# A state-space stage on one Trainium2 core: a normalization later, a copy earlier, and a prefetch's gathers split over two places

## The chip, the cores and the metric

The kernel runs on one core of a Trainium2 chip. The metric is the device time of one execution in microseconds (us), lower is better. Several executions are timed and their median is taken. One further execution was recorded by the hardware profiler, and all profile rows are from that one.

## What is computed

A two-layer decoder over `x` of 16 x 256 x 256 floats: differential attention, cross attention and a mixture of experts, then a state-space block, causal cross attention and a feed-forward block, each with a residual sum and a layer norm. The change is inside the state-space block, which is, cut to what matters:

```python
def _L1_attn_ref(x, in_proj_w, conv_w, conv_b, norm_w, out_proj_w, dt_bias, A_log, D_param):
    zxbcdt = jnp.einsum('bld,ed->ble', x, in_proj_w)
    z, xBC, dt = ...            # 512, 512 + 2 * 128 and 8 columns
    xBC = silu(causal convolution with 4 taps of xBC + conv_b)
    x_part, B_part, C_part = ...
    dt = jax.nn.softplus(dt + dt_bias)
    A = -jnp.exp(A_log)
    # for every token t: state = state * exp(A * dt_t) + (x_t * dt_t) B_t;  y_t = state C_t
    _, y_seq = lax.scan(step, state0, inputs)
    y = y + x_part * D_full
    y = y * jax.nn.silu(z)
    y = y * jax.lax.rsqrt(jnp.mean(y * y, axis=-1, keepdims=True) + EPS) * norm_w
    return jnp.einsum('ble,de->bld', y, out_proj_w)

x = _layernorm(x + _L0_ffn_ref(x, ...))     # its last sum and norm are done by this stage
x = _layernorm(x + _L1_attn_ref(x, ...))
```

## The kernel before

Each engine has one program written out by hand; an engine executes its instructions strictly in that order, and semaphores (`wait_ge`, `then_inc`) tie the engines together. The stages follow one another; the one edited here is `state_space` (L2169). In the trace its tiles carry the prefix `ssm_`.

The stage works on 16 blocks of 256 tokens (two tiles of 128 rows, `QT` = 2). The scan over tokens is not done token by token: in a block of 256 it is a product with a lower triangular matrix of decays, which is made on the fly. Every engine runs the same loop `for n in STEPS`, n from -7 to 16. In step n the core computes the state-space mix of block n, the output of block n - 1, and prepares later blocks: the projections of the next pair of blocks (eleven units B, C, x0, x1, x2, dt, x3, z0 to z3 per pair, six in an even step, five in an odd one), the transposition of block n + 4, the sum of the experts of block n + 5, and the load of block n + 7. In the loop, `now` says that block n exists, `late` that block n - 1 does, and `soon` that block n + 1 does.

The parts that the prediction speaks of, by engine:

- **PE** (TensorE): `project`, `state_products`, `exponents(n, 0..5)` (sums of logarithms that become decays, L2391 and L2392), `output(n - 1)`, `mix` (L2417 to L2419), `transpose_x`, `turn_steps` (L2360). `exponents(n, u)` for u of 2 or more waits for `decays(n, u - 2)`, as the bank of PSUM has to be free. A projection's bank is free when the unit two before it has been read.
- **ACT** (ScalarE): `decays(n, u)` (L2535) takes the exponential of a bank of exponents into tile `mat[u]`; `first_tap` (L2554) the first tap of the convolution; `normalize_x(n + 4)` (L2596) applies the layer norm to the sum of experts with `c_shift` and `c_rstd`; `normalize_y(n - 1)` (L2624) does so with the finished rows and `shift`; `copy_steps` (L2523) takes the dt unit to SBUF, for PE to turn it; `tails` (L2529) is a small exponential.
- **DVE** (VectorE): `sum_experts(n + 5)` (L2732, L2739 and the moments), `masked_products` (L2804), three more taps for each unit (L2758), the multiplications of `mat` 0, 2 and 4 with the mask (L2692), `tail_rows` (L2812), `high_terms` (L2795), `mean_squares` (L2827), `residual(n - 1)` (L2836).
- **POOL** (GpSimd): the multiplications of `mat` 1, 3 and 5 (L2692), `scale_rows` (L2985), the low terms `rhs_lo` (L2992), `scale_y` and `scale_x` (L2962 to L2967, four small instructions each, whose last one writes `shift` and `c_shift`), `split_y` (L3002, tile `y_lo`), and `gather(n + 7)` (L2954): four indirect DMAs that fetch the two routed experts' rows of a block of 256 tokens, two for each expert.

A gather's tile has three copies, and block b's gather waits until the sum of block b - 3 has been made. `sum_experts(b)` waits for all four of its block. SP (SyncE) loads the shared expert's rows of each block and stores the finished rows; it is not edited.

## Time and profile before

| | us |
|---|---|
| median of 3 runs | 2781.28 |
| lowest and highest run | 2781.17 and 2789.03 |
| the profiled execution's own time | 2787.02 |
| its span in the trace | 2784.9 |
| state space, steps 0 to 13 (starts of PE's state products, 1756.5 and 2070.4) | 313.9 |

The span is what the profiler saw from the first instruction to the last; 2.1 us lie around it. The mean granted TensorE clock over the span was 0.933 of full speed. Steps 0 to 15 lie between 1756.5 and about 2135 us of the span.

### The profile page before, as it was taken

How to read it: one execution, taken by the hardware profiler on the slowest of the kernel's cores; microseconds unless marked ns; L12 is line 12 of the kernel's file. 1: busy time of each engine (PE TensorE's matmuls, PEld its weight loads, DVE VectorE, ACT ScalarE, POOL GpSimd, SP SyncE). 2: the span in 40 equal slices, each digit the busy share in tenths (PEclk: the TensorE clock that was granted, in tenths of full speed). 3: DMA queues.
4: the chain of work that ended last, by engine and by line, in shares of the span. 5: the costliest groups of instructions: out<-in, count | busy, mean ns of one | idle time of the engine just before them, and what ended most of it. 6: DMA issues, size and time to landing. Idle time of an engine off the chain costs nothing. (4 is left out here: it accounts for less than half of the span.)

```text
span 2784.9 us, 66303 instructions
## 1 busy us (share of the span) xinstructions
PE 2455.1 (88%) x24760; PEld 2025.6 (73%) x24760; DVE 1921.6 (69%) x3087; ACT 1434.1 (51%) x2247; POOL 1564.4 (56%) x1871
## 2 busy tenths in 40 slices
PE   4899999999599998798999994888896799996998
PEld 3677666676466665798999993677775577775998
DVE  2566666677358877263888885999985377775776
ACT  2566555565246665333665663656663356553333
POOL 3565665666334553036666664777764577763443
PEclk8899999999789999799999997999997799998999
DMA  7555555552377784124666663111100877751111
GB/s 180 130 146 130 141 142 127 142 147 68 93 202 202 196 207 103 36 73 148 215 229 220 230 218 116 46 31 46 31 12 21 231 209 202 214 146 35 57 56 49
DMA packets 229623, 364.07 MB, mean 131 GB/s; under 512 B 53536, under 2 KB 158752, under 8 KB 221856
## 3 DMA queue, kind: packets, MB, share of 16 engines
q1 hardware_dynamic: 208832, 281.87, 37.7%
q0 software_dynamic: 17376, 78.13, 8.0%
q8 instruction: 153, 2.51, 0.4%
q10 hardware_dynamic: 3200, 1.05, 0.2%
q14 instruction: 62, 0.51, 0.1%
HBM read 232.27 MB, written 133.69 MB: 131 GB/s over the span
## 5 line engine op out<-in xcount | busy, mean ns | idle before, releaser
L1243 ACT ACTIVATE self_probs<-self_score_ps 128x768 f32<-128x768 f32 x256 | 207.4, 810 | 217.7 <-PE self_score_ps L1145 214.4
L1451 POOL TENSOR_SCALAR_AFFINE_SELECT self_probs<-self_probs 128x512 f32<-128x512 f32 x256 | 167.2, 654 | 217.7 <-ACT self_probs L1243 215.1
L1372 DVE TENSOR_REDUCE self_neg_max<-self_max_ps 128x2 f32<-128x256 f32 x256 | 108.0, 422 | 227.6 <-PE self_max_ps L1131 224.5
L685 DVE TENSOR_REDUCE cross_neg_max<-cross_max_ps 128x4 f32<-128x1024 f32 x128 | 156.0, 1222 | 73.1 <-PE cross_max_ps L473 71.2
L601 ACT ACTIVATE cross_probs<-cross_score_ps 128x1024 f32<-128x1024 f32 x128 | 131.0, 1024 | 93.3 <-PE cross_score_ps L495 93.0
L1373 DVE TENSOR_REDUCE self_neg_max<-self_max_ps 128x2 f32<-128x512 f32 x256 | 174.2, 680 | 0.0
L2160 POOL TENSOR_TENSOR moee_h_lo<-moee_h,moee_h_hi 128x512 fp32r<-128x512 f32 x78 | 112.0, 1436 | 92.0 <-ACT moee_h_hi L1897 91.2
L3458 POOL TENSOR_TENSOR ffn_g_lo<-ffn_g_full,ffn_g_hi 128x512 fp32r<-128x512 f32 x64 | 82.2, 1284 | 129.0 <-ACT ffn_g_hi L3344 116.6
L1145 PE MATMUL self_score_ps<-self_q_stack,self_k_stack 49*128 49x128 f32 (+1 forms) x1024 | 131.6, 336 | 23.9 <-issue 10.2
L1897 ACT ACTIVATE moee_h_hi<-moee_h 128x512 fp32r<-128x512 f32 x110 | 69.5, 632 | 160.9 <-DVE moee_h L2063 160.9
L601 ACT ACTIVATE causal_probs<-causal_score_ps 128x768 f32<-128x768 f32 x128 | 103.8, 811 | 92.1 <-PE causal_score_ps L495 92.0
L79 PE MATMUL moee_g_ps<-moee_x_hi,moee_in_hi 128*128 128x256 f32 x440 | 132.1, 300 | 9.7 <-DVE moee_x_lo L2050 5.5
L1145 PEld LDWEIGHTS self_score_ps<-self_q_stack,self_k_stack 49*128 49x128 f32 x1024 | 79.1, 191 | 73.0 <-issue 40.1
L1125 PE MATMUL self_max_ps<-self_k_stack,self_q_stack 48*128 48x128 f32 (+1 forms) x1024 | 108.7, 292 | 26.4 <-POOL self_k_stack L1482 25.5
L2063 DVE TENSOR_TENSOR moee_h<-moee_u_ps,moee_silu 128x512 f32<-128x512 f32 x110 | 75.5, 686 | 80.9 <-PE moee_u_ps L81 76.5
L2103 POOL DMA_INDIRECT x_tiles<-kept_x,moek_slot x64 | 65.2, 1019 | 109.7 <-issue 104.9
L80 PE MATMUL moee_g_ps<-moee_x_lo,moee_in_hi 128*128 128x256 f32 x440 | 126.5, 287 | 0.0
L81 PE MATMUL moee_g_ps<-moee_x_hi,moee_in_lo 128*128 128x256 f32 x440 | 126.5, 287 | 0.0
L775 POOL TENSOR_SCALAR_AFFINE_SELECT causal_probs<-causal_probs 128x512 f32<-128x512 f32 x128 | 85.6, 669 | 71.8 <-ACT causal_probs L601 68.0
L79 PE MATMUL moee_y_ps<-moee_out_hi,moee_h_hi 128*128 128x256 f32 x440 | 125.2, 284 | 0.7 <-DVE moee_out_lo L2015 0.7
L79 PE MATMUL moee_u_ps<-moee_x_hi,moee_in_hi 128*128 128x256 f32 x440 | 125.5, 285 | 0.0
L81 PE MATMUL moee_u_ps<-moee_x_hi,moee_in_lo 128*128 128x256 f32 x440 | 125.0, 284 | 0.0
(488 smaller groups left out, 9659.9 us busy)
## 6 DMA issues: line engine op xcount, KB each, us to landing
self_q<-self_q_split SPq DMA_DIRECT2D x48, 512.0 KB, 3.2
self_q_raw<-self_q SPq DMA_DIRECT2D x32, 768.0 KB, 7.4
cross_stacks<-cross_qk SPq DMA_DIRECT2D x64, 384.0 KB
causal_stacks<-causal_qk SPq DMA_DIRECT2D x64, 384.0 KB
moe_y_tiles<-moee_y SPq DMA_DIRECT2D x55, 256.0 KB, 2.4
x_tiles<-zeros SPq DMA_DIRECT2D x16, 624.0 KB, 4.5
moee_xT<-x_tiles SPq DMA_DIRECT2D x39, 256.0 KB, 7.2
cross_qk<-cross_k_split SPq DMA_DIRECT2D x16, 512.0 KB, 3.9
```

Of the source, the lines that this page charges most:

```text
L79: pe.matmul(out, a[0], b[0], start=start, stop=False, **kw)
L80: pe.matmul(out, a[0], b[1], start=False, stop=False, **kw)
L81: return pe.matmul(out, a[1], b[0], start=False, stop=stop, **kw)
L601: nc.scalar.activation(probs[i // 2][:, a, :, lo:], score_ps[:, :, lo:], ACT.Exp, scale=HD ** -0.5).then_inc(prob_ready, 1)
L685: last = dve.tensor_reduce(neg_max[p][:, tile, :, col % 4, :], bank[:].rearrange("p a (q k) -> p a q k", q=QT), AX.X, ALU.max, negate=True)
L1125: last = pe.matmul(max_ps[i % 2][:, ab, q * S:q * S + (q + 1) * P], q_stack[rows, 4 * tile + c, q * P:(q + 1) * P], k_stack[p][rows, tile, ...
L1145: last = pe.matmul(score_ps[:, ab, j * S + k * P:(j + 1) * S], k_stack[p][rows, tile, k * P:(k + 1) * P], q_stack[rows, 4 * tile + c, k * P:],
L1243: nc.scalar.activation(probs[g % 4][:, a, :, P:], score_ps[:, :, P:], ACT.Exp, scale=HD ** -0.5).then_inc(prob_ready, 1)
L1372: dve.tensor_reduce(neg_max[:, tile, :, c, 0:1], bank[:, :, 0:P], AX.X, ALU.max, negate=True)
L1373: dve.tensor_reduce(neg_max[:, tile, :, c, 1:2], bank[:, :, S:2 * S], AX.X, ALU.max, negate=True).then_inc(max_kept, 1)
L1451: pool.affine_select(diagonal, diagonal, [[0, 2], [0, 2], [1, P]], ALU.is_ge, zero, base=0, channel_multiplier=-1).then_inc(prob_masked, 1)
L2160: pool.tensor_tensor(h_lo[p][f][:].rearrange("p j s -> p (j s)"), h[f][:], h_hi[p][f][:].bitcast(F32).rearrange("p j s -> p (j s)"), ALU.s ...
```

## The change

It edits the order of the instructions of ACT and POOL in the state space. None is added or taken away, and no semaphore's count changes.

- **ACT, even steps:** `normalize_x(n + 4)` moves from ahead of `decays(n, 1)` to behind `first_tap(n, 2)`. `tails` goes from behind `decays(n, 2)` to ahead of it. `copy_steps(n)` goes ahead of `normalize_y(n - 1)`.
- **POOL, even steps with n of 0 or more:** of the four indirect DMAs of `gather(n + 7)`, the two of the first expert go between `mat` 3 and `mat` 5, the other two between the low terms and `scale_y`. They were last in the step.
- **POOL, odd steps with n of 0 or more:** the first two go behind `mat` 5, the other two to the end of the step, behind `split_y`. All four were between the second `rhs_lo` and `scale_x`.

```diff
--- before.py
+++ after.py
@@ -2632,14 +2632,14 @@
                     if now:
                         decays(n, 0)
                     first_tap(n, 1)
+                    if now:
+                        decays(n, 1)
+                        tails(n)
+                        decays(n, 2)
+                        decays(n, 3)
+                    first_tap(n, 2)
                     if real(n + 4):
                         normalize_x(n + 4)
-                    if now:
-                        decays(n, 1)
-                        decays(n, 2)
-                        tails(n)
-                        decays(n, 3)
-                    first_tap(n, 2)
                     if now:
                         decays(n, 4)
                     first_tap(n, 3)
@@ -2651,9 +2651,9 @@
                     if now:
                         upper_y(n)
                         square_y(n)
+                    copy_steps(n)
                     if late:
                         normalize_y(n - 1)
-                    copy_steps(n)
                 else:
                     if now:
                         decays(n, 0)
@@ -2945,10 +2945,12 @@
             pool.memset(neg_half[:], -0.5).then_inc(half_set, 1)
             pool.wait_ge(half_set, 1)
 
-            def gather(b):
+            def gather(b, ks=range(TOP)):
+                if not real(b):
+                    return
                 if b >= 3:
                     pool.wait_ge(sum_ready, b - 2)
-                for k in range(TOP):
+                for k in ks:
                     for q in range(QT):
                         c = b * QT + q
                         pool.indirect_dma_start(y_routed[b % 3][:, k, q, :], None, y_tiles,
@@ -3013,12 +3015,15 @@
                     matrices(pool, n, 3, high_mat_ready)
                 if n % 2 == 0:
                     if now:
+                        gather(n + 7, (0,))
                         matrices(pool, n, 5, high_mat_ready)
                     if late:
                         scale_rows(n - 1)
                     if n >= 0 and soon:
                         low_terms(n + 1, 0)
                         low_terms(n + 1, 1)
+                    if now:
+                        gather(n + 7, (1,))
                     if late:
                         scale_y(n - 1)
                     if real(n + 5):
@@ -3026,13 +3031,14 @@
                     if now:
                         split_y(n, 0)
                         split_y(n, 1)
-                    if real(n + 7):
+                    if not now:
                         gather(n + 7)
                 else:
                     if late:
                         scale_rows(n - 1)
                     if now:
                         matrices(pool, n, 5, high_mat_ready)
+                        gather(n + 7, (0,))
                     if n == -5:
                         scale_x(n + 5)
                     if n == -3:
@@ -3043,13 +3049,15 @@
                         scale_y(n - 1)
                     if soon:
                         low_terms(n + 1, 1)
-                    if real(n + 7):
+                    if not now:
                         gather(n + 7)
                     if n >= -1 and real(n + 5):
                         scale_x(n + 5)
                     if now:
                         split_y(n, 0)
                         split_y(n, 1)
+                    if now:
+                        gather(n + 7, (1,))
                     if n == -1:
                         lower_wo()
 
```

On POOL, from the end of step 2 into step 3 (odd) there stood before: `y_lo` of step 2, the four gathers, `mat` 1 and 3 of step 3, the scale of the rows, `mat` 5 and a low term:

```order
L3002 TENSOR_TENSOR ssm_y_lo<-ssm_yz,ssm_y_hi 128x512 x2
L2954 DMA ssm_y_routed<-moe_y_tiles,moek_slot 128x256 x4
L2692 TENSOR_TENSOR ssm_mat<-ssm_mat,ssm_gm 128x512 x2
L2985 TENSOR_TENSOR ssm_row_scale<-ssm_ms,ssm_neg_half 128x2
L2692 TENSOR_TENSOR ssm_mat<-ssm_mat,ssm_gm 128x512
L2992 TENSOR_TENSOR ssm_rhs_lo<-ssm_triang,ssm_a_lo 128x1024
```

The same place after the change (lines of this part of the file lie two further down):

```order
L3004 TENSOR_TENSOR ssm_y_lo<-ssm_yz,ssm_y_hi 128x512 x2
L2692 TENSOR_TENSOR ssm_mat<-ssm_mat,ssm_gm 128x512 x2
L2987 TENSOR_TENSOR ssm_row_scale<-ssm_ms,ssm_neg_half 128x2
L2692 TENSOR_TENSOR ssm_mat<-ssm_mat,ssm_gm 128x512
L2956 DMA ssm_y_routed<-moe_y_tiles,moek_slot 128x256 x2
L2994 TENSOR_TENSOR ssm_rhs_lo<-ssm_triang,ssm_a_lo 128x1024
```

Four gathers are gone from ahead of `mat` 1 and 3, and two stand behind `mat` 5.

On POOL, from the end of step 3 into step 4 (even), before, from `shift` on:

```order
L2967 TENSOR_TENSOR ssm_shift<-ssm_low,ssm_rstd 128x2
L2992 TENSOR_TENSOR ssm_rhs_lo<-ssm_triang,ssm_a_lo 128x1024
L2954 DMA ssm_y_routed<-moe_y_tiles,moek_slot 128x256 x4
L2962 TENSOR_SCALAR ssm_c_var<-ssm_c_mv 128x2
L2963 TENSOR_SCALAR ssm_c_low<-ssm_c_mv 128x2
L2965 TENSOR_TENSOR ssm_c_rstd<-ssm_c_var,ssm_neg_half 128x2
L2967 TENSOR_TENSOR ssm_c_shift<-ssm_c_low,ssm_c_rstd 128x2
L3002 TENSOR_TENSOR ssm_y_lo<-ssm_yz,ssm_y_hi 128x512 x2
L2692 TENSOR_TENSOR ssm_mat<-ssm_mat,ssm_gm 128x512 x3
```

And after the change:

```order
L2969 TENSOR_TENSOR ssm_shift<-ssm_low,ssm_rstd 128x2
L2994 TENSOR_TENSOR ssm_rhs_lo<-ssm_triang,ssm_a_lo 128x1024
L2964 TENSOR_SCALAR ssm_c_var<-ssm_c_mv 128x2
L2965 TENSOR_SCALAR ssm_c_low<-ssm_c_mv 128x2
L2967 TENSOR_TENSOR ssm_c_rstd<-ssm_c_var,ssm_neg_half 128x2
L2969 TENSOR_TENSOR ssm_c_shift<-ssm_c_low,ssm_c_rstd 128x2
L3004 TENSOR_TENSOR ssm_y_lo<-ssm_yz,ssm_y_hi 128x512 x2
L2956 DMA ssm_y_routed<-moe_y_tiles,moek_slot 128x256 x2
L2692 TENSOR_TENSOR ssm_mat<-ssm_mat,ssm_gm 128x512 x2
L2956 DMA ssm_y_routed<-moe_y_tiles,moek_slot 128x256 x2
L2692 TENSOR_TENSOR ssm_mat<-ssm_mat,ssm_gm 128x512
```

The four instructions of `scale_x` have no gather ahead of them any more; two of step 3's gathers stand between `y_lo` and `mat` 1, and two of step 4's between `mat` 3 and `mat` 5.

On ACT, an even step, as a piece of the difference: the two normalizations (L2596) fall from the second place to behind the tap of x0 (L2554 of `ssm_xs`).

```order
 L2535 ACTIVATE ssm_mat<-ssm_e_ps 128x512
 L2554 ACTIVATE ssm_bc<-ssm_in_ps,ssm_cb,ssm_cw 128x512
+L2535 ACTIVATE ssm_mat<-ssm_e_ps 128x512
+L2529 ACTIVATE ssm_tail<-ssm_g_ps 128x8
+L2535 ACTIVATE ssm_mat<-ssm_e_ps 128x512 x2
+L2554 ACTIVATE ssm_xs<-ssm_in_ps,ssm_cb,ssm_cw 128x512
 L2596 ACTIVATE ssm_x<-ssm_x,ssm_c_shift,ssm_c_rstd 128x256 x2
-L2535 ACTIVATE ssm_mat<-ssm_e_ps 128x512 x2
-L2529 ACTIVATE ssm_tail<-ssm_g_ps 128x8
-L2535 ACTIVATE ssm_mat<-ssm_e_ps 128x512
-L2554 ACTIVATE ssm_xs<-ssm_in_ps,ssm_cb,ssm_cw 128x512
```

Three `decays`, `tails` and one tap pass the normalization.

## Rows read from the trace of the kernel before

**Rows 1.** The page, part 1: busy us, share of the span, instructions

```profile
PE 2455.1 (88%) x24760; PEld 2025.6 (73%) x24760; DVE 1921.6 (69%) x3087; ACT 1434.1 (51%) x2247; POOL 1564.4 (56%) x1871
```

**Rows 2.** Stretches: us, busy us (instructions) of PE, PEld, DVE, ACT, POOL; PEclk; DMA; GB/s

```profile
1851.50:1876.90 25.40, 21.68 (x151) 18.04 (x150) 24.56 (x44) 11.67 (x19) 16.75 (x18) 0.93 0.10 29
1876.90:1901.60 24.70, 22.24 (x161) 19.08 (x159) 23.53 (x45) 18.64 (x31) 21.73 (x23) 1.00 0.21 63
...
1952.60:1979.10 26.50, 22.79 (x151) 18.89 (x150) 24.64 (x44) 11.65 (x19) 16.66 (x18) 0.87 0.08 23
...
2003.80:2027.30 23.50, 21.63 (x151) 18.04 (x149) 22.49 (x44) 11.51 (x19) 13.16 (x13) 0.93 0.00 1
```

These are the steps 4, 5, 8 and 10.

**Rows 3.** Waits from 1760 to 1970 us: total us, times, longest

```profile
PE ssm_e_ps L2391 <- ACT ssm_mat L2535: 16.8, 5, 3.8
...
ACT ssm_x L2596 <- POOL ssm_c_shift L2967: 7.3, 4, 2.1
```

**Rows 4.** Timeline of POOL, step 4: start, us, instruction [idle before]

```profile
1849.93 1.88 POOL L2954 DMA_INDIRECT ssm_y_routed<-moe_y_tiles,moek_slot  x1 [0.16 <-issue]
...
1854.81 0.95 POOL L2954 DMA_INDIRECT ssm_y_routed<-moe_y_tiles,moek_slot  x1 [0.30 <-issue]
...
1857.25 0.18 POOL L2967 TENSOR_TENSOR ssm_c_shift<-ssm_c_low,ssm_c_rstd 128x2 f32<-128x2 f32 x1
...
1866.47 1.37 POOL L2692 TENSOR_TENSOR ssm_mat<-ssm_mat,ssm_gm 128x512 f32<-128x512 f32 x1 [3.19 <-ACT ssm_mat L2535]
...
1876.36 0.22 POOL L2962 TENSOR_SCALAR ssm_var<-ssm_mv 128x2 f32<-128x2 f32 x1 [2.90 <-issue]
```

**Rows 5.** Timeline of ACT, step 4

```profile
1857.47 1.09 ACT L2596 ACTIVATE ssm_x<-ssm_x,ssm_c_shift,ssm_c_rstd 128x256 f32<-128x256 f32 x2 [1.74 <-POOL ssm_c_shift L2967]
1858.47 1.06 ACT L2535 ACTIVATE ssm_mat<-ssm_e_ps 128x512 f32<-128x512 f32 x2
```

**Rows 6.** Timeline of PE, step 4

```profile
1859.09 0.50 PE L2391 MATMUL ssm_e_ps<-ssm_rhs_hi,ssm_one_r 128*128 128x512 f32 x1 [3.72 <-ACT ssm_mat L2535]
```

**Rows 7.** Timeline of DVE, steps 4 and 5, then step 11

```profile
1859.55 2.58 DVE L2692 TENSOR_TENSOR ssm_mat<-ssm_mat,ssm_gm 128x512 f32<-128x512 f32 x2
1862.06 1.76 DVE L2812 TENSOR_TENSOR ssm_xdt_tail<-ssm_xdt,ssm_tail 128x512 f32<-128x512 f32 x1
...
1884.50 1.26 DVE L2692 TENSOR_TENSOR ssm_mat<-ssm_mat,ssm_gm 128x512 f32<-128x512 f32 x2
1885.68 0.69 DVE L2812 TENSOR_TENSOR ssm_xdt_tail<-ssm_xdt,ssm_tail 128x512 f32<-128x512 f32 x1
...
1888.57 2.38 DVE L2692 TENSOR_TENSOR ssm_mat<-ssm_mat,ssm_gm 128x512 f32<-128x512 f32 x1
...
2031.26 3.50 DVE L2692 TENSOR_TENSOR ssm_mat<-ssm_mat,ssm_gm 128x512 f32<-128x512 f32 x2
...
2038.65 0.68 DVE L2692 TENSOR_TENSOR ssm_mat<-ssm_mat,ssm_gm 128x512 f32<-128x512 f32 x1
```

**Rows 8.** Timeline of step 5: gathers, `mat`, low term on POOL; two waits of PE; DVE; ACT

```profile
1882.47 1.09 POOL L2954 DMA_INDIRECT ssm_y_routed<-moe_y_tiles,moek_slot  x1 [0.16 <-issue]
...
1887.85 2.54 POOL L2692 TENSOR_TENSOR ssm_mat<-ssm_mat,ssm_gm 128x512 f32<-128x512 f32 x2
...
1893.69 1.90 POOL L2992 TENSOR_TENSOR ssm_rhs_lo<-ssm_triang,ssm_a_lo 128x1024 fp32r<-128x1024 f32 x1 [0.90 <-DVE ssm_a_lo L2789]
...
1879.61 0.41 PE L2360 MATMUL ssm_in_ps<-ssm_ident,ahead_front 8*128 8x8 f32 x4 [0.78 <-ACT ahead_front L2523]
1891.10 0.40 PE L2417 MATMUL ssm_y_ps<-ssm_mat,ssm_xdt_tail 128*64 128x128 f32 x2 [1.61 <-DVE ssm_mat L2692]
...
1891.63 0.88 DVE L2836 SCALAR_TENSOR_TENSOR ssm_y_out<-ssm_xT_ps,ssm_row_scale,ssm_x 128x256 f32<-128x256 f32 x2 [0.68 <-issue]
...
1897.96 1.09 ACT L2624 ACTIVATE ssm_y_out<-ssm_y_out,ssm_shift,ssm_rstd 128x256 f32<-128x256 f32 x2 [0.64 <-POOL ssm_shift L2967]
```

**Rows 9.** Timeline of DVE, step 8

```profile
1965.71 2.36 DVE L2795 TENSOR_TENSOR ssm_rhs_hi<-ssm_triang,ssm_a_hi 128x1024 fp32r<-128x1024 f32 x2 [0.79 <-PE ssm_e_ps L2392]
```

## Prediction

> **What bounds the kernel now.** The page comes first: PE is busy 88% of the span and VectorE (DVE) 69% [rows 1]. Those are averages over five stages, so the stage that is edited has to be read by itself. It is the state space, and within it the steps n = 0 to 15, one block of 256 tokens each. I cut the trace at the instant at which PE starts the state products of each step. The table by stretches then shows what the reader should see [rows 2]: step 4 takes 25.4 us, of which DVE works 24.56 and PE 21.68; step 5 takes 24.7 us with DVE at 23.53. Step 2 is like step 4 (25.6 us), step 6 like step 8 (26.3 and 26.5 us), and steps 3, 5, 7 and 9 take 24.7 us each. DVE has under 2 us of idle time in any of them. So DVE is the engine that is full, and the granted TensorE clock is below 1.00 in the even steps alone.
>
> Then the waits of that stretch. ScalarE (ACT) waits four times, 7.3 us in all, for `c_shift`, which GpSimd computes, and PE waits five times, 16.8 us in all, for `mat`, which ACT computes [rows 3]. In order of time it is one chain, here in step 4. GpSimd issues the four gathers of block 10 from 1849.93 to 1855.76 and computes `c_shift` of block 8 only then, until 1857.43 [rows 4]. ACT can normalize block 8 only from 1857.47 and takes 1.09 us, and behind that stand `decays` 1 and 2 [rows 5]. PE's next exponents need `decays` 1, and start after 3.72 us of waiting, at 1859.09 [rows 6]. The granted clock is 0.93 over step 4 and 0.87 over step 8, and 1.00 over step 5 [rows 2]: a part of the even steps runs at 1.2 GHz and not at 2.4, behind the place at which PE stood still.
>
> Last, DVE's own rows, because a full engine can be full of waiting. DVE and GpSimd hold each other up when both read two tiles of SBUF. `mat` 4 of step 5 takes DVE 2.38 us, while the same instruction in step 11 takes 0.68; GpSimd worked on its own `mat` tiles at the first time [rows 7, 8]. The pair in step 4 takes 2.58 where the pair in step 5 takes 1.26, and the `xdt_tail` product 1.76 against 0.69 [rows 7]. That is 1.7 us in an odd step and 1.3 + 1.1 = 2.4 us in an even one, recorded as DVE work.
>
> The Trainium skill, page "SBUF — State Buffer", section "Who interferes with whom", says that a DVE instruction with two SBUF inputs and a GpSimd instruction that reads SBUF exclude each other for a whole instruction; by that rule, these rows agree.
>
> **The change, part by part.**
>
> *Normalization of x later on ACT (even steps).* It moves behind `decays` 1 to 3, `tails` and the first tap of x0. No instruction is added. `decays` 1 then start when their exponents and ACT are ready, right after the tap of C, and not at 1858.47, behind the wait: PE's 3.72 us wait mostly goes, and with it the slow clock. But PE is not the full engine. PE then runs up against DVE: the projection of x1 needs the taps of C, which DVE ends at 1859.55 in any case. What DVE itself gets back is its idle time. In step 8 DVE waits 0.79 us for PE's last exponents, since these came at the slow clock [rows 9]; step 6 shows 0.80 at the same place. Step 10 gathers nothing and its ACT finds `c_shift` ready; it takes 23.5 us with all of DVE's other work in it, the sum of experts included [rows 2]. It is the nearest row to what an even step becomes. I take 23.9, 0.4 us above it, since the second half of an odd step's gathers now stands right ahead of GpSimd's `mat` 1, so that it may still meet DVE's pair (as it did for 0.3 us in step 10, and for 1.3 in step 4). Steps 2, 4, 6 and 8: 1.7 + 1.5 + 2.4 + 2.6 = 8.2 us. The bounds for each: nothing, if all the collisions stay, and 2.4 + 0.4 = 2.8 us, if all go.
>
> *Gathers in the even steps.* The first pair goes between `mat` 3 and `mat` 5, where GpSimd idles 3.19 us, the second behind the low terms, where it idles 2.90 us [rows 4]. A gather is 0.95 us and 0.30 of issue, so a pair is 2.5 us and fits in either gap. Beside a DVE product of two SBUF inputs a gather took 1.88 us [rows 4]; a pair at that price is 4.4 us and makes `mat` 5 up to 1.2 us late. PE has the whole output product of the block before and the first `mix` ahead of its use, so I cost both pairs at nothing. That cover would be gone if `mat` 5 came later than DVE's `mat` 4 and the first `mix` behind it.
>
> The Trainium skill, page "SBUF — State Buffer", infers in the same section that a DVE tensor-tensor product does not hold up the building of a gather's descriptors. The 1.88 us row speaks against it; by the page the pair would be 2.5 us everywhere, and the sum the same.
>
> *Gathers gone from between `y_lo` and `mat` 1 (odd steps).* They took 5.4 us there, and pushed `mat` 3 onto DVE's `mat` 4. Without them `mat` 1 and 3 run some 4 us earlier, `mat` 4 on DVE falls back towards 0.68, and PE's 1.61 us wait for it goes [rows 7, 8]. Up to 1.7 us, and with DVE's 0.68 of idle behind it 2.4 us. Against that stand new meetings: step 11, the odd step without gathers, has the pair at 3.50, where step 5 has 1.26 [rows 7]. Step 11 has no sum of experts between `y_lo` and the pair, so the meeting is milder with one, but not gone. Between +2.4 and -2.2 us (3.50 less 1.26) a step I take +0.7, nearer to the gain, since in steps 3 to 9 the sum of experts keeps DVE away from its pair until GpSimd is nearly through `y_lo`.
>
> *Gathers placed behind `mat` 5 (first pair) and at the step's end (second pair), odd steps.* GpSimd waits 0.90 us for `a_lo` there [rows 8]; the pair takes 2.5, so the low terms, `shift` and all behind them come up to 1.6 us later. `mat` 5 comes about as much earlier, as no gathers stand ahead of it. ACT waits 0.64 us for `shift` already [rows 8]. I count nothing, with 1.6 us as the bound. Past the second pair, `c_shift` comes before the gathers and not behind them: that is the other half of the cure for ACT's wait. The gathers land a few us after issue and their sums come two steps later, so no DMA is late. SP's queue is not touched.
>
> *Steps copied ahead of the finished rows.* PE waits 0.78 us in each odd step for ACT's copy, which stood behind a 1.09 us normalization and its wait [rows 8]. The copy now comes up to 1.5 us earlier. DVE reads the turned steps only when it is free, which it was not: nothing.
>
> *Steps 0, 1 and 10* have parts of the same: 1.0 us in all.
>
> **The sum.** 8.2 + 4 x 0.7 + 1.0 = 12.0 us. Against the profiled execution's own 2787.0 us that is 2775.0. The profiled execution stood 5.7 us above the median of the three runs, 2781.3, so for the median 2781.3 - 12.0 = 2769.3 us, 0.4% less. Two of three runs lie at 2781 and one at 2789. About 0.3%, 8.3 us, is what a measurement of this kernel can tell from no change.
>
> **The rivals.**
>
> *The collisions only move.* DVE stays full, and what it no longer loses at one product it loses at the next. For it: DVE has hardly any idle time in steps 2 to 9, and step 11 has more blocked time without the gathers than step 5 with them. Against it: step 10 is 1.9 us shorter than step 4 [rows 2]. Then only the slow clock's share is won, 1.0 us in steps 6 and 8 each, and some 0.5 us in the other even steps: 4 us, 2777.3 us. Chance 0.30.
>
> *Slower: the early pair delays the turn of the step.* If `mat` 5 of the odd steps is not earlier (because `row_scale` ahead of it waits for DVE's mean squares, at the same time as before), the first pair's 1.6 us go to `shift`, then to ACT's last two gates, which free PE's banks, and to `y_lo`, which then meets the next step's sums for another 1.1 us. 2.7 us in each of steps 3, 5, 7 and 9, against 1 us won in steps 6 and 8 each: +9 us, 2790 us. It decides where `low_terms` start more than 0.9 us later behind `a_lo` than now. Chance 0.08.
>
> *Both kinds of collision go.* Each even step gives 2.8 us, steps 6 and 8 another 1.0 for the slow clock, each odd step 2.4, and steps 0, 1 and 10 together 1.2: 4 x 2.8 + 2.0 + 4 x 2.4 + 1.2 = 24 us, 2757 us. For it: the lengths of the bare products [rows 7]. Against it: GpSimd has 17 to 22 us of work in every step, and most of it reads two tiles. Chance 0.10.
>
> **How the numbers follow.** My forecast, between 9 and 17 us less, has 0.52. Faster by over 0.3% is this and the last rival: 0.62. Within 0.3% is the first rival: 0.30. Slower is the second: 0.08. The likeliest case gives 2769.3. The range runs from 2757, the case with no collisions, to 2783, which takes in the first rival and a run or two from the upper end of its spread; about 0.15 is left out.
>
> **What would show it.** Right: PE's wait for `mat` in even steps 2 to 8 at under 1.5 us, granted clock 1.00 in them, no wait of ACT for `c_shift`, even steps near 24 us, odd ones near 24. The two halves are told apart by DVE's `mat` 4 in odd steps: near 0.7 us if the gathers' place helps, near 2.4 if not. It would be wrong if the even steps stay above 25 us although PE's wait is gone (DVE then holds the pace), or if ACT's wait for `shift` in odd steps grows above 2 us.

## The result, and the profile after

The changed kernel has a median of 2793.6 us over six runs (2791.1 to 2796.5). The kernel before has 2786.1 us over six runs taken beside them (2781.2 to 2789.0), three more than were shown above. The ratio is 1.0032 (95% interval 1.0020 to 1.0045): the changed kernel is **slower by 7.5 us, 0.3%**. The forecast was 0.4% less.

The profiled execution took 2794.4 us, its span is 2792.2. Page, part 1, of the changed kernel (busy us, share of the span, instructions; against [rows 1]):

```profile
PE 2452.8 (88%) x24760; PEld 2023.7 (72%) x24760; DVE 1933.2 (69%) x3087; ACT 1434.1 (51%) x2247; POOL 1578.6 (57%) x1871
```

The same instructions keep DVE busy 11.6 us longer and POOL 14.2 us longer. Nearly all of that lies in the edited stage (10.8 and 14.6 us there); the 2.3 us that PE is busy less do not. I measure the **stage length** from GpSimd's memset at the stage's start (L2945) to DVE's first cast of the next stage (L666): 463.4 us before, 472.3 after, 8.9 more. Another execution of the changed kernel on another chip gave 472.5. The stage began between 1687.6 and 1703.6 us in the 18 traces of this study, in code that no kernel edits, so stage lengths are compared below beside the ratios. The runs of the kernel before spread over up to 21 us on one chip; where ratio and stage length say different sizes (by up to 5 us), I go by the stage.

Stretches between PE's first state products of steps 4, 5, 6, 8 and 9 of the changed kernel (columns as in [rows 2]):

```profile
1852.47:1877.20 24.73, 20.74 (x150) 16.69 (x148) 24.26 (x42) 11.43 (x18) 20.50 (x16) 1.00 0.11 33
1877.20:1905.29 28.09, 22.59 (x160) 18.98 (x159) 26.95 (x50) 18.59 (x32) 22.07 (x25) 1.00 0.16 48
1905.29:1929.19 23.90, 20.50 (x149) 16.76 (x148) 23.43 (x40) 11.43 (x18) 19.62 (x16) 1.00 0.11 33
1957.76:1981.10 23.34, 21.29 (x149) 17.75 (x148) 22.14 (x39) 11.00 (x18) 19.21 (x15) 0.95 0.09 26
1981.10:2008.15 27.05, 23.67 (x159) 20.62 (x158) 24.84 (x48) 18.95 (x32) 20.43 (x27) 0.94 0.09 30
```

The even steps became shorter and their clock is 1.00 or 0.95, not 0.93 or 0.87. The odd steps went from 24.7 to 27 or 28 us. PE's marks move against DVE's work, so the table further down cuts at DVE's own mark, the masked product (L2804): steps 2, 4, 6 and 8 then took 104.3 us before and 102.4 after, steps 3, 5, 7 and 9 took 97.9 and **107.6**. An odd step's interval holds both sums of experts, its own and that of the even step behind it.

Waits from 1760 to 1970 us of the changed kernel, total us, times, longest (against [rows 3]):

```profile
POOL ssm_row_scale L2987 <- DVE ssm_ms L2827: 25.2, 7, 4.1
...
ACT ssm_y_out L2624 <- POOL ssm_shift L2969: 15.8, 7, 3.4
...
PE ssm_in_ps L79 <- ACT ssm_zs L2591: 6.3, 3, 2.1
```

ACT no longer waits for `c_shift`, and PE's wait for ACT's `mat` is down from 16.8 to 3.5 us: what was to be cured is cured. Others stand in their place. GpSimd's for DVE's mean squares grew from 3.6 us in all to 25.2, ACT's for `shift` from 4.3 us in all and 1.0 at most to 15.8 and 3.4, and PE's for ACT's gate is new.

Timeline of POOL, step 5 of the changed kernel (start, us; against [rows 8]):

```profile
1881.87 3.00 POOL L3004 TENSOR_TENSOR ssm_y_lo<-ssm_yz,ssm_y_hi 128x512 fp32r<-128x512 f32 x2
1884.84 2.88 POOL L2692 TENSOR_TENSOR ssm_mat<-ssm_mat,ssm_gm 128x512 f32<-128x512 f32 x2
1891.85 1.07 POOL L2987 TENSOR_TENSOR ssm_row_scale<-ssm_ms,ssm_neg_half 128x2 f32<-128x2 f32 x1 [4.12 <-DVE ssm_ms L2827]
1892.88 1.27 POOL L2692 TENSOR_TENSOR ssm_mat<-ssm_mat,ssm_gm 128x512 f32<-128x512 f32 x1
1894.32 1.08 POOL L2956 DMA_INDIRECT ssm_y_routed<-moe_y_tiles,moek_slot  x1 [0.17 <-issue]
1895.71 0.96 POOL L2956 DMA_INDIRECT ssm_y_routed<-moe_y_tiles,moek_slot  x1 [0.30 <-issue]
1896.68 1.91 POOL L2994 TENSOR_TENSOR ssm_rhs_lo<-ssm_triang,ssm_a_lo 128x1024 fp32r<-128x1024 f32 x1
...
1900.98 1.09 POOL L2969 TENSOR_TENSOR ssm_shift<-ssm_low,ssm_rstd 128x2 f32<-128x2 f32 x1
1902.03 2.88 POOL L2994 TENSOR_TENSOR ssm_rhs_lo<-ssm_triang,ssm_a_lo 128x1024 fp32r<-128x1024 f32 x1
```

Timeline of DVE, steps 5 and 6 of the changed kernel:

```profile
1881.33 0.55 DVE L2804 TENSOR_TENSOR ssm_gm<-ssm_g_ps,ssm_triang 128x384 f32<-128x384 f32 x1
...
1883.75 2.83 DVE L2739 SCALAR_TENSOR_TENSOR ssm_x<-ssm_y_routed,moek_weight,ssm_y_shared 128x256 f32<-128x256 f32 x2
...
1891.69 0.68 DVE L2692 TENSOR_TENSOR ssm_mat<-ssm_mat,ssm_gm 128x512 f32<-128x512 f32 x1
...
1903.07 2.51 DVE L2732 SCALAR_TENSOR_TENSOR ssm_y_shared<-ssm_y_routed,moek_weight,ssm_y_shared 128x256 f32<-128x256 f32 x2
...
1907.49 0.53 DVE L2804 TENSOR_TENSOR ssm_gm<-ssm_g_ps,ssm_triang 128x384 f32<-128x384 f32 x1
...
1912.37 3.32 DVE L2692 TENSOR_TENSOR ssm_mat<-ssm_mat,ssm_gm 128x512 f32<-128x512 f32 x2
1915.60 0.68 DVE L2812 TENSOR_TENSOR ssm_xdt_tail<-ssm_xdt,ssm_tail 128x512 f32<-128x512 f32 x1
1916.20 2.35 DVE L2795 TENSOR_TENSOR ssm_rhs_hi<-ssm_triang,ssm_a_hi 128x1024 fp32r<-128x1024 f32 x2
1918.47 1.76 DVE L2692 TENSOR_TENSOR ssm_mat<-ssm_mat,ssm_gm 128x512 f32<-128x512 f32 x1
```

With the same rows of the kernel before they give step 5's account:

```profile
1882.63 0.88 DVE L2739 SCALAR_TENSOR_TENSOR ssm_x<-ssm_y_routed,moek_weight,ssm_y_shared 128x256 f32<-128x256 f32 x2
...
1901.92 0.86 DVE L2732 SCALAR_TENSOR_TENSOR ssm_y_shared<-ssm_y_routed,moek_weight,ssm_y_shared 128x256 f32<-128x256 f32 x2
```

In step 5, `y_lo` starts 0.1 us behind DVE's first sum instruction and not 1.1 us ahead of it, and GpSimd's `mat` 1 and 3 (1884.84) run right behind it, where the gathers stood. Together they fall on L2739, the second half of DVE's sum, which takes 2.83 us for 0.88: `y_lo` holds the first of its two instructions, `mat` 1 the second. Behind the early pair the second low term is late (1902.03) and falls on the next sum: 2.51 for 0.86. `mat` 4 is won, 0.68 for 2.38 [rows 7]. That is 1.95 + 1.65 - 1.70 = **+1.9 us**. DVE's gate (L2867) took 1.66 us for 1.21 and its `rhs_hi` 2.34 for 3.00, which leaves 1.7 us; the step went from 24.5 to 26.2 us (L2804 at 1881.33 and 1907.49). In the even step 6 the `mat` pair takes 3.32 us, the tail 0.68 and `mat` 4 1.76, 5.76 in all; before, these three took 2.58, 1.76 and 0.68, 5.02.

Step 9 is another matter. It takes 28.4 us, 24.5 before, and it issues no gather in any kernel, as there is no block 16. Its products are those of step 5 up to `mat` 4. Then the granted clock falls while PE makes the output and the transposes. Stretches of the changed kernel and of the variant "`shift` first" of the next section, each 11.8 or 11.2 us behind the step's masked product:

```profile
1997.00:2003.00 6.00, 6.00 (x54) 5.60 (x51) 4.69 (x16) 1.08 (x2) 4.78 (x7) 0.72 0.01 3
1993.00:1999.00 6.00, 5.99 (x65) 5.30 (x66) 5.33 (x17) 1.80 (x4) 4.78 (x7) 1.00 0.01 3
```

At the mean clock of 0.72 PE has 54 matmuls on record in place of 65, DVE waits for it, and its gate and next sum then meet GpSimd (2.28 us for 1.22, 2.94 for 0.87). With the same products up to `mat` 4 and the clock at 1.00 the step takes 24.7 us. So **3.7 of the 8.9 us** are this one fall of the clock, at the same place in both executions of the changed kernel. Four kernels have it in step 9 (28.4 to 28.7 us): the changed one, "ScalarE's, GpSimd's even steps", "wait for the sum" and "gathers at the head only". The second and the fourth have no early pair. What decides whether the clock falls there, no run shows.

### The profile page after: what moved, and what is told of

It reads as the page before. It is cut to its first block and busy times, and to the rows that moved or that the text cites. A ratio compares the mean times of both kernels' runs of the same rounds, so it can differ in the third digit from the quotient of the medians.

```text
span 2792.2 us, 66303 instructions
## 1 busy us (share of the span) xinstructions
PE 2452.8 (88%) x24760; PEld 2023.7 (72%) x24760; DVE 1933.2 (69%) x3087; ACT 1434.1 (51%) x2247; POOL 1578.6 (57%) x1871
## 3 DMA queue, kind: packets, MB, share of 16 engines
q8 instruction: 153, 2.51, 0.4%
## 5 line engine op out<-in xcount | busy, mean ns | idle before, releaser
L601 ACT ACTIVATE cross_probs<-cross_score_ps 128x1024 f32<-128x1024 f32 x128 | 131.1, 1024 | 91.6 <-PE cross_score_ps L495 91.4
L80 PE MATMUL moee_u_ps<-moee_x_lo,moee_in_hi 128*128 128x256 f32 x440 | 125.6, 285 | 0.0
```

The costliest lines, as they stand in the source:

```text
L80: pe.matmul(out, a[0], b[1], start=False, stop=False, **kw)
L601: nc.scalar.activation(probs[i // 2][:, a, :, lo:], score_ps[:, :, lo:], ACT.Exp, scale=HD ** -0.5).then_inc(prob_ready, 1)
```

## The experiments

Each kernel below was timed beside the kernel before on the same chip, in four groups of four. "Products" is DVE's time in the stage for its six kinds of instruction with two SBUF inputs (L2692, L2795, L2812, L2867, L2732, L2739), each as its mean by its full count. "Even" is steps 2, 4, 6 and 8 together, "odd" is 3, 5, 7 and 9, cut at L2804.

| kernel | ratio to before (95%) | stage us | even | odd | products |
|---|---|---|---|---|---|
| before | 1 | 463.4 | 104.3 | 97.9 | 173.2 |
| changed | 1.0032 (1.0020 to 1.0045) | 472.3 | 102.4 | 107.6 | 183.9 |
| changed, again | 1.0027 (1.0017 to 1.0038) | 472.5 | 102.4 | 107.6 | 183.8 |
| ScalarE's part alone | 1.0006 (0.9991 to 1.0021) | 468.0 | 104.9 | 97.9 | 180.5 |
| GpSimd's part alone | 1.0052 (1.0033 to 1.0072) | 478.4 | 105.8 | 104.1 | 178.8 |
| ScalarE's, GpSimd's even steps | 1.0012 (1.0000 to 1.0024) | 468.9 | 100.5 | 104.2 | 178.3 |
| ScalarE's, GpSimd's odd steps | 1.0019 (1.0003 to 1.0034) | 469.6 | 101.7 | 103.3 | 179.8 |
| wait for the sum | 1.0046 (1.0031 to 1.0061) | 474.6 | 102.0 | 109.2 | 184.6 |
| `shift` first | 1.0021 (1.0011 to 1.0031) | 466.5 | 102.6 | 102.7 | 181.2 |
| spaced | 0.9972 (0.9959 to 0.9984) | 456.9 | 96.6 | 100.2 | 164.0 |
| spaced, ScalarE as before | **0.9962** (0.9945 to 0.9978) | **453.0** | 96.5 | 96.5 | 159.0 |
| spaced, later normalization only | 0.9980 (0.9965 to 0.9996) | 453.9 | 95.9 | 97.3 | 159.9 |
| waits only | 1.0012 (0.9998 to 1.0025) | 463.0 | 103.5 | 97.9 | 161.0 |
| gathers at the head only | 1.0045 (1.0027 to 1.0064) | 471.5 | 106.7 | 101.9 | 182.4 |
| short `mat`: before | 0.9952 (0.9937 to 0.9967) | 449.5 | 101.9 | 90.2 | 147.7 |
| short `mat`: changed | 0.9913 (0.9887 to 0.9939) | 442.1 | 91.6 | 96.0 | 152.8 |
| short `mat`: `shift` first | 0.9932 (0.9910 to 0.9955) | 444.9 | 93.7 | 94.9 | 152.8 |
| short `mat`: GpSimd's part alone | 0.9944 (0.9927 to 0.9962) | 444.7 | 95.0 | 95.8 | 147.9 |

**The parts by themselves.** From the changed kernel, first GpSimd's program set back, then ScalarE's, then the odd and the even branch of GpSimd's loop.

> ACT's part alone: x normalized later, steps copied ahead, GpSimd's order as before. Meetings theory (the loss comes from GpSimd's products meeting DVE's sums of experts once the gathers are out of their way): DVE's two sum instructions stay as in the kernel before (13.3 and 9.7 us over the steps), PE's wait for mat in the even steps goes, and the time is 0 to 4 us under before. Delay theory (the loss comes from the first pair of an odd step's gathers, which makes shift late for ACT): the same, as that pair is not moved. Were ACT's part itself the loss, it would be 5 to 9 us above before.

> GpSimd's part alone, ACT's order as before. Meetings theory: the sums take about 20 and 17 us as in the changed kernel, and the time is at or above the changed kernel's, 7 to 14 us over before. Delay theory: ACT's wait for shift in odd steps above 2 us and the same time. If the two parts only harm together, it is within 3 us of before.

> ACT's part and the split of the gathers in even steps; odd steps keep all four gathers ahead of scale_x. Meetings theory: mat 1 and 3 follow y_lo at once in odd steps, the sums take 17 to 20 us each, and most of the loss is here: 4 to 8 us over before. Delay theory: the pair in odd steps is not behind mat 5, ACT waits 0.6 us for shift, and the time is at or below act_only.

> ACT's part and the split of the gathers in odd steps; even steps keep all four gathers at their end. Meetings theory: the four gathers still stand between y_lo and mat 1 of the odd steps, DVE's first sums of the stretch stay short, and the time is within 3 us of act_only. Delay theory: ACT's wait for shift is 2 to 3.5 us in each odd step, PE waits some 2 us for the third z, and most of the loss is here: 4 to 8 us over before.

ScalarE's part alone was expected at 0 to 4 us under before, or 5 to 9 above; its ratio doesn't differ from 1, and its stage is 4.6 us longer. Neither part is good alone, and they don't add: 4.6 and 15.0 us of stage length by themselves, 8.9 together. With ScalarE's part alone PE's stall is gone and the clock is 1.00 in steps 4, 6 and 8, and yet the even steps take 26.2 us each, no less in all than before: GpSimd's products meet DVE's `rhs_hi` instead (its share of the products is 52.9 us for 47.5), and the products take 7.3 us more. The two branches of GpSimd's part, each added to ScalarE's, cost another 0.9 us (even) and 1.6 us (odd); with both it is 4.3. Step 9's fall of the clock is in the first and in the last of these numbers. Without its 3.7 us the even branch gains 2.8 us, the odd one costs 1.6, and both together cost 0.6.

**The meeting with the sum.** Ahead of `mat` 1 in odd steps:

```diff
+                if now and n % 2 and real(n + 5):
+                    pool.wait_ge(sum_ready, n + 6)
                 if now:
                     matrices(pool, n, 1, high_mat_ready)
```

> The changed kernel once more, as a base for the runs beside it. Every theory: the stage as in its first trace, 472 us against 463 of the kernel before, DVE's products of two SBUF inputs at 184 us (counts filled up) against 173.

> The changed kernel; in odd steps GpSimd waits, ahead of mat 1, until DVE has made the sum of experts of this step. Meetings theory: the second sum instruction falls from 24 us to about 15.4, and the stage is 4 to 8 us shorter than the changed kernel's. Delay theory (shift late behind the pair of gathers): the wait makes GpSimd no earlier anywhere, the stage stays at 472 or grows.

L2739 fell from 24.1 to 19.1 us, and DVE's `mat` rose from 51.5 to 57.8: a part of the meeting was moved on to the next product, and the stage is 2.1 us longer than the changed kernel's on this chip (472.5). L2739 did not fall to the 15.4 us of the kernel before, because `y_lo` still holds its first instruction. One wait at one meeting isn't a cure.

**The early pair.** In the odd steps `gather(n + 7, (0,))` goes from behind `mat` 5 to behind `scale_y(n - 1)`.

> The changed kernel; in odd steps the first pair of gathers goes behind scale_y. Delay theory: ACT's waits for shift fall from up to 3.4 to about 1 us, PE's wait for the gates of z goes (6.3 us), and the stage is 4 to 8 us shorter. Meetings theory: DVE's sums stay at 26 and 24 us and the stage changes by under 3 us.

Against the changed kernel on the same chip the stage is 5.9 us shorter, the odd steps are 4.9, ACT's wait for `shift` fell from 19.4 to 11.5 us (1750 to 2118 us), and PE's for ACT's gate went. The timed ratios, 1.0021 and 1.0027, can't be told apart. Most of the 5.9 us isn't the pair's: steps 9 and 10, which issue no gather, are 5.2 us shorter, 3.7 of them the clock of step 9. Steps 0 to 8, in whose odd ones the pair was moved, are 1.1 us shorter in all, step 3 not at all, steps 5 and 7 by 0.5 and 0.7. Timeline of POOL, step 5, of this kernel:

```profile
1892.46 1.90 POOL L2994 TENSOR_TENSOR ssm_rhs_lo<-ssm_triang,ssm_a_lo 128x1024 fp32r<-128x1024 f32 x1 [0.89 <-DVE ssm_a_lo L2789]
...
1895.84 0.86 POOL L2969 TENSOR_TENSOR ssm_shift<-ssm_low,ssm_rstd 128x2 f32<-128x2 f32 x1
```

The wait for `a_lo` is back at 0.89 us. `shift` is done 17.9 us behind the step's masked product (1878.76), as before the change (17.7), and not 20.7. What that brings in step 5 is the gate, 1.22 us for 1.66. The second low term comes no earlier, as the pair now stands right ahead of it, and the sums stay nearly as dear as they were (L2732 24.4 us for 26.5, L2739 24.1 in the stage), and with them the odd steps' other 4.8 us.

**Without GpSimd's `mat` products.** A leave-out: they multiply 128x2 elements and not 128x512, and take 17.2 us in all in place of 69.6. First in both kernels, then in two variants.

```diff
+            if ready is high_mat_ready:
+                eng.tensor_tensor(mat[:, u, 0, 0:2], mat[:, u, 0, 0:2], gm[:, u // 2, 0:2],
+                                  ALU.mult).then_inc(ready, 1)
+                return
```

> A leave-out: GpSimd's mat 1, 3 and 5 multiply 128x2 elements each and not 128x512, so its 48 products take some 5 us instead of 60 or more, and the values in them stay unmasked. Everything else is the kernel before. DVE's own mat products (L2692) should fall towards their bare length, 48 x 0.65 = 31 us from 50 or so. It is the yardstick for the next run. Both theories: stage 445 to 455 us.

> The same leave-out in the changed kernel. The changed kernel is 8.9 us longer than the kernel before. If its cost is the late shift and the gathers' own delays in the odd steps (5.9 us by the run with the pair moved back), this one is longer than short_before by 5 to 7 us. If it is meetings of DVE's products with GpSimd's mat products, the difference is under 2 us, or the changed kernel is the shorter one. In between, each has its share.

> GpSimd's mat products cut to 128x2 elements as in the last, GpSimd's gathers as in the changed kernel, ScalarE as before the change. With ScalarE's part the even steps 2 to 8 took 91.6 us in all and the stage 442.1; with neither part 101.9 and 449.5. If the later normalization makes the even steps short, they stay near 101 us here and the stage is 447 to 452 us. If the gathers' places do it (c_shift is early now in any case), they are 92 to 95 us and the stage is within 2 us of 442.

> The changed kernel with GpSimd's mat products cut to 128x2 elements, and the first pair of the odd steps behind the scale of y. Without that move the shortened kernel has 96.0 us in steps 3, 5, 7 and 9 and a stage of 442.1 us. If the pair's delay of shift is what the odd steps lose, they fall to 90 to 92 us and the stage to 436 to 438 us. If the loss belongs to the second pair or to ScalarE's copy, both stay within 1.5 us.

This turned the sign. With short products the changed order is **7.4 us shorter** than the old one, not 8.9 longer: even steps 91.6 against 101.9 us, odd ones 96.0 against 90.2. The 48 products of GpSimd cost the old order 13.9 us of stage length and the new one 30.2; step 9's fall of the clock, which went with them, is in the second number. The stretches of steps 4, 5 and 6, first of the old order with short products:

```profile
1849.31:1874.92 25.61, 21.84 (x150) 17.99 (x149) 22.70 (x44) 11.73 (x19) 13.31 (x18) 0.93 0.10 31
1874.92:1897.41 22.49, 21.70 (x160) 18.85 (x159) 21.32 (x45) 18.39 (x31) 18.15 (x24) 1.00 0.22 64
1897.41:1922.93 25.52, 21.74 (x149) 17.95 (x148) 22.68 (x44) 11.72 (x19) 13.78 (x18) 0.93 0.09 28
```

and of the changed order with them, steps 5 and 6:

```profile
1865.53:1889.01 23.48, 22.00 (x160) 18.77 (x159) 22.35 (x45) 18.12 (x31) 16.20 (x22) 1.00 0.18 54
1889.01:1911.08 22.07, 20.56 (x150) 16.69 (x149) 21.60 (x42) 11.31 (x18) 16.62 (x17) 1.00 0.11 33
```

In the old order step 6 stays at 25.5 us though DVE works only 22.68 of it: the chain through `c_shift`, with the slow clock behind it (0.93), is a bound of its own. The new order takes it away, to 22.07 us at a clock of 1.00. Without ScalarE's part the even steps are 95.0 us, so the gathers' places alone do two thirds of that (6.9 of 10.3 us), and ScalarE's part the rest. Moving the early pair back did not help here (444.9 against 442.1 us, odd 94.9): that the pair's delay is what the odd steps lose falls for this kernel. The short products leave out meetings and some 50 us of GpSimd's work at once, and can't tell the two apart.

**Spacing.** ScalarE's part as in the change; all four gathers at the head of each step, and then GpSimd waits until DVE is past its own pair:

```diff
                 if now:
+                    gather(n + 7)
+                    if n % 2:
+                        pool.wait_ge(xtail_ready, n + 1)
+                    else:
+                        pool.wait_ge(low_mat_ready, 3 * n + 3)
                     matrices(pool, n, 1, high_mat_ready)
                     matrices(pool, n, 3, high_mat_ready)
```

> ACT as in the changed kernel; on GpSimd all four gathers at the head of every step, then a wait until DVE is through its tail product (odd steps) or its last mat (even steps), then mat 1 and 3. Meetings theory: GpSimd's products run beside DVE's taps, DVE's products of two SBUF inputs fall below the 173 us of the kernel before, even steps to 23 to 24 us, and the stage is 5 to 15 us shorter than before. If mat 1, 3 and 5 come too late for the second mix, PE waits for GpSimd's mat there and the stage is longer than before. Delay theory: shift waits go as in the run above, and the stage is 4 to 8 us shorter than the changed kernel's.

Then the same with ScalarE's part undone, with the normalization's half of it alone, and each half of GpSimd's edit added to the kernel before by itself.

> The spaced kernel with ScalarE's order as in the kernel before. In the state-space stage the spaced kernel took 456.9 us, the kernel before 463.4 and the one with ScalarE's part alone 468.0. If ScalarE's part costs only because it lets GpSimd's products start onto DVE's, it should be worth something here, where GpSimd waits for its place: PE's wait for mat in the even steps (3.7 us each) comes back, and the stage is longer than 458.5 us, 461 to 463 by my estimate, ratio to before 0.999. If ScalarE's part is bad or idle by itself, the stage is 456 us or shorter, and the 6.5 us are all GpSimd's.

> The spaced kernel with the later normalization alone, the copy of the steps where it was before. ScalarE's part costs 3.9 us there (456.9 against 453.0). If the later normalization costs it (it delays nothing that DVE needs, but brings PE's and GpSimd's work closer to DVE's products), the stage is 456 to 458 us. If the earlier copy costs it (it pushes the normalization of y, and GpSimd's y_lo behind it, in the odd steps), the stage is 452 to 454 us.

> The kernel before with nothing but the two waits of the spaced kernel on GpSimd ahead of mat 1 (DVE's tail rows in odd steps, DVE's mat 4 in even ones); gathers and ScalarE as before. If the waits make the gain, the six two-input products of DVE fall from 173.2 to under 168 us and the stage is 457 to 460 us. If it is the gathers at the head of the step that matter, the products stay above 170 us and the stage stays at 463 us or grows, since GpSimd has its gathers ahead of mat 1 and again nothing to do while it waits.

> The kernel before with nothing but all four gathers moved to the head of each step, ahead of mat 1; no waits, ScalarE as before. With the waits and this place the stage took 453.0 us, with the waits alone 463.0, before 463.4. If the place does the work (c_shift no longer behind the gathers, so ScalarE's normalization and PE's exponents come early), the stage is 453 to 456 us. If each part is hidden behind what the other removes, it is 458 to 463 us and DVE's six products stay above 168 us.

The two halves make a square of stage lengths: 463.4 before, 463.0 with the waits, 471.5 with the gathers' place, **453.0 with both**. Each alone gives nothing or harm; the gathers alone are worse than either expectation had it, and about half of their 8.1 us is step 9, where the clock fell as in the changed kernel (28.4 us). Timeline of DVE, POOL and PE in an even step with the waits alone (step 4):

```profile
1862.01 1.51 DVE L2692 TENSOR_TENSOR ssm_mat<-ssm_mat,ssm_gm 128x512 f32<-128x512 f32 x2
...
1867.67 3.77 POOL L2692 TENSOR_TENSOR ssm_mat<-ssm_mat,ssm_gm 128x512 f32<-128x512 f32 x3 [5.31 <-DVE ssm_mat L2692]
...
1861.55 0.50 PE L2391 MATMUL ssm_e_ps<-ssm_rhs_hi,ssm_one_r 128*128 128x512 f32 x1 [3.72 <-ACT ssm_mat L2535]
```

and its steps 4 and 6 as stretches:

```profile
1854.00:1877.76 23.76, 20.04 (x150) 16.85 (x149) 22.42 (x43) 11.09 (x18) 15.25 (x16) 1.00 0.11 32
...
1903.18:1928.51 25.33, 21.60 (x150) 18.00 (x148) 22.40 (x42) 11.07 (x18) 15.25 (x16) 0.93 0.09 25
```

DVE's products are cheap now, but PE still waits 3.72 us, and in step 6 DVE works only 22.40 of 25.33 us: what the waits gave went into idle time behind the old chain. Most of that is the slow clock. Step 4, with the same wait and the same DVE work but the clock at 1.00, is 1.6 us shorter. With the gathers at the head alone it is the other way round. Timeline of its even step 4:

```profile
1874.17 4.63 DVE L2812 TENSOR_TENSOR ssm_xdt_tail<-ssm_xdt,ssm_tail 128x512 f32<-128x512 f32 x1
...
1874.49 3.75 POOL L2692 TENSOR_TENSOR ssm_mat<-ssm_mat,ssm_gm 128x512 f32<-128x512 f32 x3
```

GpSimd has all three `mat` to do in one go and DVE's tail (0.69 us bare, [rows 7]) waits for the whole of it. With both halves, step 4 of the best kernel, DVE then POOL:

```profile
1856.63 1.32 DVE L2692 TENSOR_TENSOR ssm_mat<-ssm_mat,ssm_gm 128x512 f32<-128x512 f32 x2
1857.88 0.68 DVE L2812 TENSOR_TENSOR ssm_xdt_tail<-ssm_xdt,ssm_tail 128x512 f32<-128x512 f32 x1
1858.48 2.35 DVE L2795 TENSOR_TENSOR ssm_rhs_hi<-ssm_triang,ssm_a_hi 128x1024 fp32r<-128x1024 f32 x2
1860.75 0.68 DVE L2692 TENSOR_TENSOR ssm_mat<-ssm_mat,ssm_gm 128x512 f32<-128x512 f32 x1
...
1868.32 2.44 DVE L2867 TENSOR_TENSOR ssm_yz<-ssm_yz,ssm_zs 128x1024 f32<-128x1024 f32 x1
...
1861.51 3.77 POOL L2692 TENSOR_TENSOR ssm_mat<-ssm_mat,ssm_gm 128x512 f32<-128x512 f32 x3 [3.33 <-DVE ssm_mat L2692]
```

The step's four products are bare, and one meeting is left, the gate at 2.44 us for 1.22. An even step takes 24.1 us in the mean. This kernel beats both: 2776.3 us against 2784.9 beside it, 0.38% less (0.22 to 0.55%).

ScalarE's part is worth nothing here. The stage was 3.9 us longer with it, 0.9 with the later normalization alone. The other 3.0 us are no cost of the copy that these runs show: step 5 took 28.2 us for 24.5, which is more than all of them, and in it the clock fell at the place where it falls in step 9 of the changed kernel. Stretches of step 5, spaced and then with the later normalization only:

```profile
1888.00:1893.00 5.00, 5.00 (x52) 4.78 (x49) 4.14 (x15) 0.06 (x1) 3.85 (x5) 0.66 0.02 5
1892.40:1897.40 5.00, 4.93 (x57) 4.24 (x54) 4.69 (x16) 1.09 (x2) 3.85 (x5) 1.00 0.02 5
```

The ratios of the three spaced kernels overlap, so their order is read from one trace each.

## Why the prediction was wrong

**What bounds the kernel: right, and incomplete.** DVE was full, the chain through `c_shift` was there, and the slow clock stood behind it. The chain, with the slow clock behind it, is a second limit next to DVE's and not a feature of the first: waits alone, gathers alone and short products in the old order each ran into the one that was left.

**Even steps, 8.2 us: measured 1.9.** The step that failed is "It is the nearest row to what an even step becomes", step 10. What should happen on PE did: clock 1.00 in steps 4 and 6, no wait for `c_shift`. But step 10 has no gathers at all, and the changed steps have four. They put `mat` 1 and 3 on DVE's pair (3.32 us in step 6) and `mat` 5 on DVE's `mat` 4 (1.76). "So that it may still meet DVE's pair" was in the text, at 0.4 us; in step 6 the pair alone is 2.1 us over its bare 1.26. ScalarE's part alone shows it without any moved gather: no stall, clock 1.00, and 26.2 us a step. The rival "the collisions only move" held for these steps. That 24 us was within reach is shown by the spaced kernels (24.1) and by the short products (22.9).

**Odd steps, 0.7 us gained in each: measured 2.4 lost on average,** 2.1, 1.7 and 1.9 in steps 3, 5 and 7 and 4.0 in step 9. Two terms failed, and a fall of the clock that no term foresaw has 3.7 of step 9's 4.0 us. The first is "since in steps 3 to 9 the sum of experts keeps DVE away from its pair". It does, and pays for it, as the sum's two instructions read two SBUF tiles as well: L2739 takes 2.83 us for 0.88. I had priced the pair and `mat` 4, and `mat` 4 came as forecast (0.68), but the sum wasn't in the account. The lower bound, -2.2 us, held in steps 3, 5 and 7 and not in step 9. The second is "I count nothing, with 1.6 us as the bound", with "`mat` 5 comes about as much earlier". It doesn't: `row_scale` stands ahead of it and waits 4.12 us for DVE's mean squares, and `mat` 5 is done 12.8 us behind the masked product, before 12.6. So `low_terms` start 1.9 us later, and `shift` is done 3.0 us later. The second number is above the bound because `shift`'s four small instructions met DVE's products on their way (1.09 us each for two of them, `var` and `shift`).

**The second rival, "the early pair delays the turn of the step", came near the time by luck.** Its condition was met (`low_terms` more than 0.9 us later, measured 1.9), as could be read from the order: `row_scale`, which waits for DVE, stood ahead of `mat` 5 all along. Its time was 2790 us at a chance of 0.08, the measured median 2793.6. But it priced the delay at 2.7 us in each of four steps, and with the pair moved back steps 5 and 7 gave 0.5 and 0.7 us, step 3 nothing, and step 9 has no pair. What made the kernel slower is the sum's meeting in the odd steps, less what `mat` 4 and the even steps gave (5.2 of the 8.9 us together with the pair's delay), and the clock in step 9 (3.7).

**Steps 0, 1 and 10, 1.0 us gained: measured 2.2 lost,** 1.5 of them in step 1, where the sum meets `mat` 1 too (L2739 1.87 us for 0.97).

**Gathers in the even steps, nothing: wrong.** "That cover would be gone if `mat` 5 came later than DVE's `mat` 4": it starts at 1918.26 us, with DVE's `mat` 4 at 1918.47, and blocks it. A gather beside DVE's `rhs_hi` took 1.99 us again:

```profile
1914.68 1.26 POOL L2956 DMA_INDIRECT ssm_y_routed<-moe_y_tiles,moek_slot  x1 [0.16 <-issue]
1916.25 1.99 POOL L2956 DMA_INDIRECT ssm_y_routed<-moe_y_tiles,moek_slot  x1 [0.30 <-issue]
1918.26 1.43 POOL L2692 TENSOR_TENSOR ssm_mat<-ssm_mat,ssm_gm 128x512 f32<-128x512 f32 x1
```

The Trainium skill, page "SBUF — State Buffer", section "Who interferes with whom", infers that building descriptors isn't held up by such a product; this row, like [rows 4], is against it.

**Steps copied earlier:** PE's wait of 0.78 us went, as said, and it gave nothing.

## What to carry to other kernels

Compare stages step by step, with the granted clock beside each step: one step of 28 us made up two fifths of this loss and most of what one variant seemed to gain. Where two engines block each other, list for each stretch every instruction on either side that takes part, with its bare and its blocked length, before moving anything. A gap filled on one of them moves all that follows it onto the other's next product. Look for the second limit before pricing the removal of the first: here the chain and the blocked products each hid the other's gain, and only the two edits together, early gathers and a wait that keeps GpSimd off DVE's products, gave 10.4 us. A helper engine that is told to wait 3 us can be worth more than one that is kept busy.

## What the runs showed of the hardware

- A DVE scalar_tensor_tensor with two SBUF inputs takes part in the blocking as a plain product does: 2.83 us for 0.88, 2.51 for 0.86.
- A product can be held for a run of the other engine's instructions, not for one: DVE's tail, 0.69 us bare, took 4.63 us beside three GpSimd products issued back to back (3.75 us), and ended 0.6 us behind the last of them.
- A mean granted clock of 0.72 over 6 us of PE's output work made a step of 24.7 us one of 28.4, as the products that follow then meet GpSimd's at another place. With the same 3.72 us wait of PE an even step took 26.3 us at a clock of 0.93 or 0.94 and 24.7 at 1.00 (waits only).
- Instructions of GpSimd with only 128x2 elements pay for a whole product of DVE: 1.09 us for 0.18 to 0.23.
- The length of the stage repeated within 0.2 us in two executions of the changed kernel, while the start of the stage moved by up to 16 us between traces.
